# Each engine takes the stages of five software-pipelined streams in its own order

## The chip, the cores and the metric

The kernel runs on one core of a Trainium2 chip. The metric is the device time of one execution in microseconds, lower is better; the time before is the median of three runs. The core has five engines with a queue each: TensorE (PE, matmuls into PSUM), VectorE (DVE), ScalarE (ACT), GpSimd (POOL, and issuer of some DMAs) and SyncE (SP, issuer of most DMAs). They meet only through semaphores.

## The reference

Two transformer layers over x of shape (16, 256, 256). With `xn = layernorm(x)`:

```
layer 0: x = x + attention(xn) (16 heads of 16, causal, x @ w_qkv, softmax, @ w_out)
               + qffn(xn)      (W = (codes - 128) * scale; down(silu(gate) * up), hidden 704)
layer 1: x = x + latent attention(xn) (16 heads, latent 64 with its own layernorm, causal softmax)
               + moe(xn)       (32 experts of 96, top 6 of sigmoid scores, and a shared expert of 192)
```

## The kernel before

One element of the batch (256 tokens by 256) is the unit of work; there are 16. Its work is cut into stages, and five streams of stages run at once, each on another element. In a steady run `it` they are, with the digit that selects them in the string:

- 0, `xx1(it)`, layer 0, 44 stages: `stack` (DVE copies the stacked query and key parts), `q0` to `q7` (score rows for the row maxima), `f0` to `f2` (quantised ffn chunks), `q8` to `q15`, `max`, `f3` to `f5`, `dn5`, `k0` to `k15` (scores again, exponentials, weighing), `w3`, `t1`, `end`.
- 1, `xx2(it-1)`, layer-1 attention and router, 31 stages: `O1` (turn the loaded layer-0 attention output), `OP` (output projection, new x), `LN`, `X` (turn the normalised x), `GRAM` (and router logits), `K`, `RS` (and values), `ROUTER`, `COMB` (turn and store the expert weights), `LOAD`, `Q0` to `Q7` (two score rows each), `MAX`, `K0` to `K7` (two key rows each), `W3`, `T1`, `O`, `PROJ`.
- 2, `xx3(it-2, last_units)`, the experts' later half: gates `g`, ups `u` and downs `d` of units 7 to 13, then `OUT`. "Older" in what follows, written `<g8`.
- 3, `xx3(it-1, first_units)`, units 0 to 6 ("newer", `>g0`); unit 0 and 1 are the shared expert, and `>wt` is the stage in which GpSimd broadcasts the expert weights with 12 DMAs.
- 4, `xx0(it+1)`, layer 0's front, 6 stages: `ln1`, `x` (turn), `qq`, `kk`, `v`, `land` (SP loads the stacked parts).

`xx` is `sp`, `gp`, `act`, `dve` or `pe`. Each of these is a Python generator that emits its engine's part of a stage and yields. A stage may be empty on an engine. `run` walks the string and calls `next` on the stream that each digit names; what it emits lands in the engine's queue in that order:

```
def run(layer1, layer0, older, newer, front, order="body"):
    streams = (layer0, layer1, older, newer, front)
    for turn in ORDERS[order]:
        if streams[int(turn)] is not None:
            next(streams[int(turn)], None)
```

There are five strings of 125 digits, one for each kind of run: `start` (it 0, with the last weight pieces and folding as streams 2 and 3), `first` (it 1), `body` (it 2 to 14, 13 runs), `late` and `end`. All five engines use the same string.

PSUM is what ties the engines together: two banks for stream 0 and 4 (`ring1`), two for stream 1 (`ring2`), two for the experts (`ring3`, bank 0 for gates and bank 1 for ups), and two accumulators. TensorE fills a bank, ScalarE, VectorE or both empty it. An expert unit goes PE gate, ACT tanh (L921), DVE product (L1224), POOL times the broadcast weights (L712), PE up, DVE product (L1219), ACT high half (L917), POOL low half (L721), PE down (L1341). SP's `>g0` loads `xe`, once the older stream's last up is done; GpSimd's `>g0` adds the bias into `xbe` (L698), once SP has stored the `xbe` of the element before (L555, stage `<OUT`).

Of the kernel before, what the change touches and what calls it, by code (L numbers as in the profile page):

```python
# [65 lines left out]
def prev(it):  # L66

    if isinstance(it, int):
# [11 lines left out]
ORDERS = {  # L80
    "body": ("022022100112201001002102212122210122022201021021211111031030201023100101011011301000043303"
             "41000040303043003433043310303331033"),
    "start": ("202021002020010013011200020010000020122110001302003330310110014122403301020123243321233111"
             "00413013103132204412213010313230110"),
    "first": ("001001210022121001310311210200003200131101012010310221013031012311321013114201302300100401"
             "20300400224122000324203204303330332"),
    "late": ("042220120012120421011220121220021224202201111114210212131020301020131330013014310011010300"
             "03300303000003034000001000333133331"),
    "end": ("200001021210212120122441220400012200212221040022020110001110002001021131423031021330101304"
             "11300101310331333133031003000330303"),  # L90
# [3 lines left out]
def program(nc, a, out):  # L94
# [22 lines left out]
    with ctx:  # L117
# [442 lines left out]
        def _(sp):  # L560
# [71 lines left out]
            run(None, None, None, None, front)  # L632
            for i in range(NSLOT, NCODE):
                load_codes(i)
            run(None, sp1(sp, 0), convert(1, EARLY), None, sp0(sp, 1), order="start")
            run(sp2(sp, 0), sp1(sp, 1), convert(EARLY, len(pieces)), sp3(sp, 0, first_units), sp0(sp, 2), order="first")
            for it in range(2, B - 1):
                run(sp2(sp, it - 1), sp1(sp, it), sp3(sp, it - 2, last_units), sp3(sp, it - 1, first_units), sp0(sp, it + 1))
            run(sp2(sp, B - 2), sp1(sp, B - 1), sp3(sp, B - 3, last_units), sp3(sp, B - 2, first_units), None, order="late")
            run(sp2(sp, B - 1), None, sp3(sp, B - 2, last_units), sp3(sp, B - 1, first_units), None, order="end")  # L640
            run(None, None, sp3(sp, B - 1, last_units), None, None)
# [84 lines left out]
        def _(gp):  # L726
# [37 lines left out]
            run(None, None, None, None, gp0(gp, 0))  # L764
            run(None, gp1(gp, 0), convert(1, EARLY), None, gp0(gp, 1), order="start")
            run(gp2(gp, 0), gp1(gp, 1), convert(EARLY, len(pieces)), gp3(gp, 0, first_units), gp0(gp, 2), order="first")
            for it in range(2, B - 1):
                run(gp2(gp, it - 1), gp1(gp, it), gp3(gp, it - 2, last_units), gp3(gp, it - 1, first_units), gp0(gp, it + 1))
            run(gp2(gp, B - 2), gp1(gp, B - 1), gp3(gp, B - 3, last_units), gp3(gp, B - 2, first_units), None, order="late")
            run(gp2(gp, B - 1), None, gp3(gp, B - 2, last_units), gp3(gp, B - 1, first_units), None, order="end")  # L770
            run(None, None, gp3(gp, B - 1, last_units), None, None)
# [154 lines left out]
        def _(act):  # L926
# [24 lines left out]
            run(None, None, None, None, front)  # L951
# [13 lines left out]
            run(None, act1(act, 0), convert(1, EARLY), folding(), act0(act, 1), order="start")  # L965
            run(act2(act, 0), act1(act, 1), convert(EARLY, len(pieces)), act3(act, 0, first_units), act0(act, 2), order="first")
            for it in range(2, B - 1):
                run(act2(act, it - 1), act1(act, it), act3(act, it - 2, last_units), act3(act, it - 1, first_units), act0(act, it + 1))
            run(act2(act, B - 2), act1(act, B - 1), act3(act, B - 3, last_units), act3(act, B - 2, first_units), None, order="late")
            run(act2(act, B - 1), None, act3(act, B - 2, last_units), act3(act, B - 1, first_units), None, order="end")  # L970
            run(None, None, act3(act, B - 1, last_units), None, None)
# [258 lines left out]
        def _(dve):  # L1230
# [75 lines left out]
            run(None, None, None, None, front)  # L1306
# [18 lines left out]
            run(None, dve1(dve, 0), convert(1, EARLY), folding(), dve0(dve, 1), order="start")  # L1325
            run(dve2(dve, 0), dve1(dve, 1), convert(EARLY, len(pieces)), dve3(dve, 0, first_units), dve0(dve, 2), order="first")
            for it in range(2, B - 1):
                run(dve2(dve, it - 1), dve1(dve, it), dve3(dve, it - 2, last_units), dve3(dve, it - 1, first_units), dve0(dve, it + 1))
            run(dve2(dve, B - 2), dve1(dve, B - 1), dve3(dve, B - 3, last_units), dve3(dve, B - 2, first_units), None, order="late")
# [423 lines left out]
```

## Time and profile before

| | before |
|---|---|
| median of 3 runs | 2086.21 us (2081.82 to 2092.85) |
| profiled execution | 2090.68 us |
| its span, first to last instruction | 2088.9 us |
| mean granted clock of TensorE | 0.971 |
| TensorE, VectorE, GpSimd, ScalarE busy | 84%, 53%, 42%, 39% |
| one steady run | about 121 us |
| bytes moved by DMA | 139.26 MB, 67 GB/s |

A busy share is the union of an engine's recorded instructions. Matmuls are recorded with their pipeline, so that neighbours overlap. A granted clock of 1.00 is full speed.

### The profile page before, as it was taken

To read this page: it belongs to the slowest core of one execution; us is meant where nothing else is said; L and a number is where in the kernel's file an instruction comes from. 1 tells how busy PE (TensorE), PEld (TensorE's weight loads), DVE (VectorE), ACT (ScalarE), POOL (GpSimd) and SP (SyncE) were. 2 spreads that over 40 slices of the span, in tenths; PEclk is the share of its full clock that TensorE was granted. 3 is DMA by queue.
4 is the path that set the end of the run, shared out by engine and by line. 5 is a ranking of instruction groups with operands and counts; after the bars stand their busy time and mean duration, and the time that the engine had idled before them with its cause. 6 is when DMAs were issued, how large, how long until landed. Compare 5 with 4: busy or idle time off the path is not lost.

```text
span 2088.9 us, 41844 instructions
## 1 busy us (share of the span) xinstructions
PE 1758.0 (84%) x16112; PEld 1337.9 (64%) x16112; DVE 1108.2 (53%) x2557; ACT 822.3 (39%) x1598; POOL 875.5 (42%) x995
## 2 busy tenths in 40 slices
PE   3647888889898888989888898988889898888887
PEld 2424666757676575766767576776757677676666
DVE  5546373645547365563736556473645547364432
ACT  2433425343342534334353433425343343534432
POOL 2323334534354353435435343534534353443445
PEclk7778999999999999999999999999999999999999
DMA  6532212313141231314123141412313141321111
GB/s 142 132 91 60 69 44 70 73 49 74 40 94 50 65 72 55 74 40 93 50 68 75 49 74 40 98 45 75 68 48 74 45 104 40 81 56 44 52 57 36
DMA packets 323318, 139.26 MB, mean 67 GB/s; under 512 B 227568, under 2 KB 308528, under 8 KB 323120
## 3 DMA queue, kind: packets, MB, share of 16 engines
q1 hardware_dynamic: 304688, 86.23, 18.2%
q0 software_dynamic: 18432, 50.36, 9.0%
q8 instruction: 128, 2.10, 0.4%
q14 instruction: 70, 0.57, 0.1%
HBM read 102.12 MB, written 29.88 MB: 63 GB/s over the span
## 4 chain that ended last, share of the span: by engine, by line
PE 29%; DVE 23%; ACT 13%; issue 12%; POOL 10%; SPq 7%; DMA 5%; DVEq 0%; POOLq 0%; ACTq 0%
PE s3r L1344 7%; POOL gs L712 4%; SPq L529 3%; POOL cb L691 3%; DVE th L1219 3%; DVE gs L1224 3%; PE s2acc L1341 3%; ACT p L826 2%; DVE m L1174 2%; PE s2r L1559 2%; PE s1a L1344 2%; ACT th L921 2%; POOL h2l L721 2%; PE s1acc L1447 2%; ACT p L886 2%
## 5 line engine op out<-in xcount | busy, mean ns | idle before, releaser
L721 POOL TENSOR_TENSOR h2l<-th,h2h 128x512 f16<-128x512 f32 (+1 forms) x224 | 246.8, 1102 | 388.6 <-ACT h2h L917 385.2
L712 POOL TENSOR_TENSOR gs<-gs,cb 128x512 f32<-128x512 f32 x192 | 243.4, 1268 | 309.8 <-DVE gs L1224 306.2
L917 ACT CAST h2h<-th 128x512 f16<-128x512 f32 (+1 forms) x224 | 131.6, 588 | 542.4 <-DVE th L1219 501.1
L1344 PE MATMUL s3r<-xe,xg 128*128 128x256 f16 x2304 | 285.3, 274 | 1.6 <-DVE gs L1224 0.5
L1344 PE MATMUL s3r<-xe,xu 128*128 128x256 f16 x2304 | 283.6, 273 | 0.4 <-DVE th L1219 0.4
L1341 PE MATMUL s2acc<-xd,h2h 128*128 128x256 f16 x1536 | 264.7, 274 | 13.5 <-POOL h2l L721 13.5
L1224 DVE SCALAR_TENSOR_TENSOR gs<-th,s3r 128x512 f32<-128x512 f32 (+1 forms) x224 | 144.9, 647 | 234.8 <-ACT th L921 234.3
L1344 PEld LDWEIGHTS s3r<-xe,xg 128*128 128x128 f16 x2304 | 223.5, 98 | 38.3 <-issue 6.6
L1344 PEld LDWEIGHTS s3r<-xe,xu 128*128 128x128 f16 x2304 | 225.6, 98 | 27.3 <-DVE th L1219 1.0
L691 POOL DMA_DIRECT2D cb<-comb_d x384 | 227.6, 600 | 20.3 <-issue 10.6
L1219 DVE TENSOR_TENSOR th<-s3r,gs 128x512 f32<-128x512 f32 x192 | 132.4, 690 | 170.9 <-POOL gs L712 157.4
L1341 PE MATMUL s2acc<-xd,h2l 128*128 128x256 f16 x768 | 210.7, 274 | 0.0
L921 ACT ACTIVATE th<-s3r 128x512 f32<-128x512 f32 (+1 forms) x224 | 126.3, 564 | 199.8 <-PE s3r L1344 198.1
L1341 PEld LDWEIGHTS s2acc<-xd,h2h 128*128 128x128 f16 x1536 | 148.7, 98 | 38.3 <-POOL h2l L721 20.1
L1174 DVE TENSOR_REDUCE m<-s2r 128x3 f32<-128x384 f32 x256 | 130.8, 551 | 14.0 <-PE s2r L1561 8.2
L886 ACT ACTIVATE p<-s2r 128x384 f32<-128x384 f32 x256 | 111.1, 486 | 62.7 <-PE s2r L1605 62.7
L656 POOL TENSOR_TENSOR h1p<-th,h1p 128x256 f16<-128x256 f32 x96 | 64.4, 670 | 130.4 <-ACT h1p L814 129.7
L1559 PE MATMUL s2r<-stacks 126*128 126x128 f16 (+1 forms) x512 | 85.6, 253 | 29.5 <-DVE m L1174 13.5
L698 POOL TENSOR_TENSOR xbe<-x,bo_row 128x512 f32<-128x512 f32 x16 | 21.8, 1364 | 199.3 <-DMA out<-xbe 199.3
L1052 DVE TENSOR_REDUCE mx<-s1b 128x2 f32<-128x512 f32 x128 | 87.1, 681 | 16.8 <-PE s1b L1423 16.8
L826 ACT ACTIVATE p<-s1b 128x512 f32<-128x512 f32 x128 | 76.6, 599 | 44.7 <-PE s1b L1466 38.9
L1052 DVE TENSOR_REDUCE mx<-s1a 128x2 f32<-128x512 f32 x128 | 87.1, 681 | 10.8 <-PE s1a L1423 10.8
(280 smaller groups left out, 3157.6 us busy)
## 6 DMA issues: line engine op xcount, KB each, us to landing
cb<-comb_d POOLq DMA_DIRECT2D x128, 192.0 KB, 3.4
part_d<-part SPq DMA_DIRECT2D x32, 512.0 KB, 3.2
cb<-comb_d POOLq DMA_DIRECT2D x128, 128.0 KB, 3.1
stacks<-part_d SPq DMA_DIRECT2D x192, 64.0 KB, 2.4
va<-v_d SPq DMA_DIRECT2D x512, 8.0 KB
cb<-comb_d POOLq DMA_DIRECT2D x128, 64.0 KB, 3.1
land<-part_d SPq DMA_DIRECT2D x96, 64.0 KB, 2.7
part<-part_d SPq DMA_DIRECT2D x96, 64.0 KB, 4.0
```

Of the source, the lines that this page charges most:

```text
L691: gp.dma_start(dst, src[which, 2 * group:2 * group + 2].partition_broadcast(32 * count)).then_inc(sem(f"cb2_loaded{group % 2}"), 16)
L712: g.tensor_tensor(gc2[:, p % 2, :], gs2[:, p % 2, :], cb2[:, 2 * (p % 6):2 * (p % 6) + 2, :].rearrange("p a s -> p (a s)"), ALU.mult).then ...
L721: g.tensor_tensor(h2l[0:m, n % 2, 0:w], th2[0:m, n % 2, 0:w], h2h[0:m, n % 2, 0:w], ALU.subtract).then_inc(sem("h2l_made"), 1)
L886: s.activation(p2[:, i % PSLOT, :], ring2[u % 2][:, 0:3 * P], ACT.Exp, scale=L ** -0.5).then_inc(empties2(u), 1)
L917: s.copy(h2h[0:m, n % 2, 0:w], th2[0:m, n % 2, 0:w]).then_inc(sem("h2h_made"), 1)
L921: s.activation(th2[0:m, n % 2, 0:w], ring3[0][0:m, 0:w], ACT.Tanh, scale=0.5).then_inc(sem("th2_made"), 1)
L1052: v.tensor_reduce(mx1[:, h, :], two(bk), AX.X, ALU.max).then_inc(empties1(u), 1)
L1174: v.tensor_reduce(m32[:, h, :], bk[:, 0:3 * P].rearrange("p (c n) -> p c n", n=P), AX.X, ALU.max).then_inc(empties2(u), 1)
L1219: ins = v.tensor_tensor(th2[0:m, s, 0:w], bk[0:m, 0:w], gc2[0:m, s, 0:w], ALU.mult)
L1224: v.scalar_tensor_tensor(gs2[0:m, s, 0:w], th2[0:m, s, 0:w], 1.0, ring3[0][0:m, 0:w], ALU.add, ALU.mult).then_inc(empties3(0), 1)
L1341: ins = nc.tensor.matmul(bk, lhs[i][k], rhs[j][k], start=first and chain[0], stop=last and chain[1], skip_group_check=True)
L1344: ins = nc.tensor.matmul(bk, lhs[i][k], rhs[j][k], start=first, stop=last)
```

## The change

`ORDERS` gets a level above: a dictionary of the five strings for each engine, and `run` takes the engine's name. Every string still has each digit as often as before (44, 31, 23, 21 and 6 times), so each stream's own stages keep their sequence; only how the streams interleave on one engine changes, separately for each. Stages, waits, buffers and transfers are the same.

```
-def run(layer1, layer0, older, newer, front, order="body"):
+def run(engine, layer1, layer0, older, newer, front, order="body"):
     streams = (layer0, layer1, older, newer, front)
-    for turn in ORDERS[order]:
+    for turn in ORDERS[engine][order]:
...
-    "body": ("022022100112201001002102212122210122022201021021211111031030201023100101011011301000043303"
-             "41000040303043003433043310303331033"),
+  "pe":  "body": ("022020012122001121002101022221120220212100142212101012131301200103100101031101310120001003"
+                  "34300300403040003043343303001333133"),
+  "dve": "body": ("020202011120012120010212122020212212012102021211120121130103001100001000303003010112100002"
+                  "44033040340330331030314303310333431"),
...
```

The body string in stage names, as far as an engine has work in the stage. Before, all engines (stages with TensorE work, then VectorE's):

```
PE  <g7 <u7 q0 <d6 <g8 O1 q1 q2 OP <u8 <d7 q3 X q4 q5 GRAM q6 q7 <g9 K f0 <u9 <d8 RS <g10 <u10 <d9 <g11 COMB f1 <u11 <d10 f2 <g12 <u12
    <d11 q8 Q0 q9 <g13 Q1 q10 <u13 Q2 <d12 Q3 Q4 Q5 Q6 Q7 q11 >g0 MAX q12 >u0 q13 <d13 q14 K0 q15 >g1 K1 max f3 K2 f4 K3 f5 K4 K5 dn5
    K6 K7 >u1 k0 W3 k1 k2 k3 k4 >d0 k5 >g2 x T1 k6 k7 k8 k9 qq k10 >u2 k11 >d1 k12 kk >g3 k13 k14 >u3 v >d2 >g4 k15 >u4 >d3 O w3 >g5 t1
    >u5 >d4 >g6 PROJ >u6 >d5
DVE stack <g7 <u7 q0 <g8 O1 q1 q2 OP LN <u8 q3 X q4 q5 GRAM q6 q7 <g9 K f0 <u9 RS <g10 ROUTER <u10 <g11 f1 <u11 f2 <g12 <u12 q8 Q0 q9
    <g13 Q1 q10 <u13 Q2 Q3 Q4 Q5 Q6 Q7 q11 >g0 MAX q12 >u0 q13 q14 q15 <OUT >g1 max f3 f4 f5 dn5 K7 >u1 ln1 >g2 x T1 qq >u2 k12 kk ...
```

After, each engine's own:

```
PE  <g7 <u7 q0 <d6 q1 q2 O1 <g8 OP <u8 <d7 q3 q4 X <g9 GRAM q5 q6 <u9 K q7 RS f0 <d8 <g10 <u10 <d9 COMB <g11 f1 <u11 <d10 f2 <g12 <u12
    Q0 q8 q9 Q1 <d11 <g13 Q2 <u13 Q3 q10 Q4 q11 Q5 <d12 Q6 >g0 Q7 >u0 q12 MAX <d13 q13 q14 K0 q15 >g1 K1 max f3 K2 f4 K3 f5 >u1 K4 K5 dn5
    K6 K7 k0 W3 k1 k2 k3 T1 k4 k5 >d0 >g2 x >u2 k6 k7 >d1 k8 k9 qq k10 >g3 k11 kk k12 k13 k14 >u3 k15 v >d2 >g4 >u4 >d3 w3 >g5 t1 O
    >u5 >d4 >g6 PROJ >u6 >d5
DVE stack <g7 q0 <u7 q1 q2 O1 OP LN <g8 q3 q4 X <u8 GRAM q5 q6 K q7 <g9 RS <u9 ROUTER <g10 f0 <u10 f1 <g11 <u11 f2 Q0 <g12 Q1 q8 <u12
    q9 Q2 <g13 Q3 Q4 Q5 <u13 q10 Q6 Q7 MAX >g0 q11 q12 >u0 q13 q14 q15 max f3 f4 f5 dn5 >g1 >u1 K7 <OUT ln1 x >g2 qq k12 >u2 kk ...
ACT ... <g9 K RS <u9 <g10 f0 COMB <u10 f1 <g11 f2 <u11 ... (before: <g9 K f0 <u9 RS <g10 <u10 <g11 COMB f1 <u11 f2)
POOL ... <u13 f3 f4 f5 dn5 >g0 >u0 >u1 >wt >g2 ... (before: <u13 >g0 >u0 f3 f4 f5 dn5 >u1 >wt >g2)
SP  ... COMB LOAD >g0 q8 q9 q10 q11 q12 q13 MAX q14 q15 max ln1 <OUT kk ... (before: COMB LOAD q8 to q11 >g0 MAX q12 to q15 <OUT max ln1 kk)
```

## Rows read from the trace of the kernel before

**Rows 1.** The page's totals: busy time, share of the span and instructions of each engine.
```profile
PE 1758.0 (84%) x16112; PEld 1337.9 (64%) x16112; DVE 1108.2 (53%) x2557; ACT 822.3 (39%) x1598; POOL 875.5 (42%) x995
```

**Rows 2.** Stretches of the span, first two and last from the edges, middle steady.
```profile
core 0: us, PE busy (x) PEld busy (x) DVE busy (x) ACT busy (x) POOL busy (x), PEclk, DMA share, GB/s
0.00:152.50 152.50, 76.86 (x463) 47.40 (x464) 78.30 (x170) 55.10 (x90) 39.55 (x43) 0.75 0.53 125
152.50:276.60 124.10, 99.36 (x870) 71.80 (x869) 68.71 (x156) 47.30 (x93) 43.44 (x52) 0.92 0.23 59
...
962.39:1083.43 121.04, 106.69 (x1004) 82.00 (x1004) 66.42 (x155) 49.23 (x97) 52.55 (x60) 1.00 0.27 65
...
1930.00:2050.00 120.00, 103.58 (x961) 80.65 (x962) 50.33 (x119) 43.98 (x83) 58.00 (x66) 0.99 0.19 54
```

**Rows 3.** TensorE's waits in seven steady runs: total us, times, longest.
```profile
PE s2r L1580 <- ACT p L886: 15.6, 14, 1.2
PE s2r L1547 <- DVE cm L1166: 12.3, 7, 1.8
PE s2r L1344 <- DVE part L1096: 7.7, 7, 1.4
PE s1b L1464 <- DVE x1l L1021: 6.9, 7, 1.0
PE s1a L1421 <- DVE kst L1041: 6.7, 7, 1.0
PE s2r L1344 <- DVE part L1110: 5.9, 7, 0.8
...
PE s1acc L1447 <- ACT p L826: 4.5, 14, 0.4
...
PE s2r L1350 <- DVE xn L996: 3.7, 7, 0.5
PE s2r L1559 <- DMA stacks<-part_d: 3.6, 7, 0.9
PE s2r L1602 <- DMA stacks<-mt: 2.8, 7, 0.7
```

**Rows 4.** TensorE in a steady run, in order of time: start, length, instruction.
```profile
1024.13 1.47 PE L1344 MATMUL s3r<-xe,xg 128*128 128x256 f16 x12
1025.44 1.47 PE L1344 MATMUL s3r<-xe,xu 128*128 128x256 f16 x12
...
1031.03 0.33 PE L1559 MATMUL s2r<-stacks 126*128 126x128 f16 x2
...
1031.31 0.33 PE L1559 MATMUL s2r<-stacks 126*128 126x128 f16 x2
...
1069.89 0.39 PE L1341 MATMUL s2acc<-shd,h2h 128*128 128x256 f16 x2
```

**Rows 5.** VectorE in the same steady run, in order of time.
```profile
1014.63 0.67 DVE L1224 SCALAR_TENSOR_TENSOR gs<-th,s3r 128x512 f32<-128x512 f32 x1
...
1034.61 6.53 DVE L1174 TENSOR_REDUCE m<-s2r 128x3 f32<-128x384 f32 x12
...
1046.78 0.68 DVE L1207 TENSOR_TENSOR xbe<-s2acc,xbe 128x512 f32<-128x512 f32 x1
...
1062.54 0.62 DVE L1010 TENSOR_TENSOR xn<-s2r,rc 128x64 f32<-128x64 f32 x4
```

**Rows 6.** GpSimd in the same steady run, in order of time.
```profile
1050.72 1.27 POOL L698 TENSOR_TENSOR xbe<-x,bo_row 128x512 f32<-128x512 f32 x1 [14.15 <-DMA out<-xbe]
1051.95 0.67 POOL L721 TENSOR_TENSOR h2l<-th,h2h 128x256 f16<-128x256 f32 x1
...
1066.45 7.15 POOL L691 DMA_DIRECT2D cb<-comb_d  x12
```

**Rows 7.** DMA issues of SP: count, size, median us to landing.
```profile
xe<-part SPq DMA_DIRECT2D x16, 256.0 KB, 2.4
out<-xbe SPq DMA_DIRECT2D x16, 256.0 KB, 2.2
```

More of the change, by code:

```diff
@@ L80 @@
 ORDERS = {
-    "body": ("022022100112201001002102212122210122022201021021211111031030201023100101011011301000043303"
-             "41000040303043003433043310303331033"),
[L83 to L88, printed above, removed]
@@ new lines @@
+    "pe": {
+        "body": ("022020012122001121002101022221120220212100142212101012131301200103100101031101310120001003"
+                 "34300300403040003043343303001333133"),
+        "start": ("200201120110120100000311100022002402000120001030001130103323023312204102130041332101330121"
+                 "01243103103221023312234302140103101"),
+        "first": ("022010021102100103021222321110030200120031110101301010130210103121131301110103201033401024"
+                 "32002004201204200303043402003323323"),
+        "late": ("022212010204014222120101000212201222121202210211103121114023410300301011001003131343243011"
+                 "00100300100300100300300003033331333"),
+        "end": ("201402014122212100022001212002201021201022402020140420001002110001003131000100201321310431"
+                 "31031331313103313023001301303013330"),
+    },
@@ new lines @@
+    "act": {
+        "body": ("022201120101200122100122021011210221002022210010121123202131130010021012011130101300104030"
+                 "34000040040303034403333300310333331"),
+        "start": ("002220101022010020003110200000201121000101002023001130011301301413322411010313201031410323"
+                 "03131122340113212220034133020303204"),
+        "first": ("221100001212131020010121003221111020210030120001100300230121123011131210213213020120413003"
+                 "04120000243023204001004334003033333"),
+        "late": ("212000120022001100221102221212210222201100122001413212101311023110430314000411320311010400"
+                 "03330100040301003003001033333133030"),
+        "end": ("100222211121102212412201120221202202214141000211103203124304410010103000000310100301311200"
+                 "00233301000333133001130030303031300"),
+    },
@@ new lines @@
+    "gp": {
+        "body": ("002122114002200422020210202012222420011102201410002100020010033434003303301301203301011200"
+                 "11101313013300210013333311013103101"),
+        "start": ("201201132403211000002003030011103000213020023310400420300021123210111022010131304121010241"
+                 "03100010312231302131110024032333022"),
+        "first": ("220013020000101220013432200030012112011400011121001211002131210300003114210031313102002400"
+                 "02323002132340030312132313340302011"),
+        "late": ("201000400221000212112120422221212402212121211022203120210100031013001403043303303330031010"
+                 "03103310000130100004311311000303113"),
+        "end": ("202020020220122022001020020012021012241121222313000112333000101033101313030010031030241014"
+                 "13100340341033011200134331131100001"),
+    },
@@ L950, in _ @@
             piece(0)
-            run(None, None, None, None, front)
+            run("act", None, None, None, None, front)
             for i in range(NCODE):
@@ L1305, in _ @@
             v.tensor_scalar(centre[:, :], ident[0:L, 0:L], 1.0 / L, None, ALU.subtract).then_inc(sem("dve_const"), 1)
-            run(None, None, None, None, front)
+            run("dve", None, None, None, None, front)
             for i in range(NCODE):
@@ L1674, in _ @@
             pe.wait_ge(*event("acc_cleared", None, 2))
-            run(None, None, None, None, pe0(pe, 0))
+            run("pe", None, None, None, None, pe0(pe, 0))
             for i in range(NCODE):
```

89 lines of the change are left out of this document (55 added, 34 removed).

## The prediction

> **What bounds the kernel now.** I read the engine totals first, then the busy time run by run, then TensorE's waits in the steady runs, and only then the order of instructions around each wait. TensorE leads with 84% [rows 1]. Single runs say more: a steady run takes 121.04 us, in which TensorE is busy 106.69 us, VectorE 66.42, GpSimd 52.55 and ScalarE 49.23, at a granted clock of 1.00, the 2.4 GHz level [rows 2]. Thirteen such runs are 1,573 us of the 2088.9, so the body string decides nearly everything. TensorE is the bound, but 121.04 - 106.69 = 14.35 us of each run it stands still, and only that can be won by an order, since no instruction is added or removed. The waits of seven steady runs tell what it stands for: the ten rows shown make 69.7 / 7 = 10.0 us per run in pieces of 0.4 to 2.2, so no one chain holds TensorE [rows 3]. So the question is, place by place, whether the new string puts more ready work between a producer and TensorE's need of it, and what it delays in exchange.
>
> Some prices serve all of it. One expert pass (gate, up or down, twelve matmuls) holds TensorE 1.31 us, the distance of two such starts, 1024.13 and 1025.44; a layer-1 query row (half a stage) holds it 0.28 us, the distance of 1031.03 and 1031.31; a layer-0 row is three matmuls, about 0.33 us by a quarter of 1.31 [rows 4]. A 512-column VectorE step takes 0.67 us [rows 5].
>
> **The change part by part, body run.** No stage gets a new wait, DMA or table load; every number below is a changed distance.
>
> COMB. TensorE waits 12.3 / 7 = 1.76 us for the router's weights [rows 3]. VectorE now does the router before older gate 10, not after: 0.67 us earlier [rows 5]; it also does ffn 0 (two steps of half the columns, 0.7 us) after it. TensorE has between RS and COMB: before, gate 10, up 10, down 9, gate 11, 4 x 1.31 = 5.2 us; after, ffn 0 (eight matmuls, 0.87), down 8, gate 10, up 10, down 9, 6.1 us. Sum: 0.67 + 0.7 + 0.9 = 2.3 us of room against a wait of 1.76. I count the whole 1.76 as gone.
>
> OP. It waits 7.7 / 7 = 1.10 us for the low part of O1 [rows 3]. Before, two layer-0 query rows (0.66 us) lie between O1 and OP; after, older gate 8 (1.31). Gain 0.65; I add 0.2 since VectorE no longer does gate 8 ahead of O1: 0.85.
>
> X and GRAM. X waits 3.7 / 7 = 0.53 for the layernorm and gets a second query row in front (0.33): gain 0.33. GRAM waits 5.9 / 7 = 0.84 [rows 3]; the two query rows (0.66) in front of it become gate 9 (1.31): gain 0.65. Against them, VectorE now does OP and the whole layernorm before older gate 8, and TensorE's gate 9 needs that bank. Up 8, down 7, q3, q4 and X cover 3.8 us; the new x (0.68), the layernorm of nine short steps (an estimate of 3 us, between four and five full steps) and the product (0.67) take 4.4: loss 0.3 with X's remaining wait counted as cover.
>
> x (front). The key row behind it waits 6.9 / 7 = 0.99 for its low part [rows 3]. Newer up 2 (1.31) moves between them and the turn T1 (four matmuls, 0.45) moves away, to between k3 and k4: gain 0.75 there and, since T1, down 1 and kk now stand before the fourth, eighth and twelfth key rows, most of the 4.5 / 7 = 0.64 for the exponentials: 0.4.
>
> The query block. This is the one stretch where VectorE sets the pace: it takes twelve maxima without a gap in 6.53 us, 0.54 each, while TensorE needs 0.28 per row [rows 4, 5]. Q3 to Q7 stand back to back in the old string, and five stages cost TensorE 10 x 0.54 = 5.4 us instead of 2.8. In the new one q10, q11, down 12 and newer gate 0 are strewn among them, and VectorE does the older output sum and newer gate 1 and its step after this stretch (0.69 + 0.4 us less in it). I read 1.1 us from what leaves VectorE here and 0.4 from the load wait of 3.6 / 7 = 0.51 [rows 3], since ScalarE copies COMB before gate 11, not after: 1.5 together. The most it could be is 2.6 + 0.5.
>
> Costs. MAX to K0: before q12, up 0, q13, down 13, q14 cover (3.1 us), after only down 13, q13, q14 (2.0), with a wait there already of 2.8 / 7 = 0.40 [rows 3]; VectorE answers sooner by q11 and gate 0 (about 0.5): loss 0.6. Newer gate 0 needs a load that SP issues after older up 13; it lands 2.4 us after its issue [rows 7], and the cover shrinks from 7 to about 4 us: loss 0.2. On SP that issue now stands ahead of the value loads of q8 to q15, sixteen DMAs that nobody needs before k0. The output sum moves on VectorE behind K7 and its store on SP behind the load of x: GpSimd's xbe, idle 14.15 us for it, runs later, and newer down 0 waits for GpSimd. Worked out from rows: the tail of K7 ends at 1062.54 + 0.62, the sum takes 0.68, the store 2.2 to land, xbe 1.27, the low part 0.67: 1068.0, and 0.9 more estimated for the hops between four queues, 1068.9, against down 0 at 1069.89 [rows 4 to 7]: it fits with 1.0 us to spare, less as TensorE gets faster: loss 0.3. Twelve broadcasts of 7.15 us follow on GpSimd [rows 6], 4 us later than now, and gate 2's product after them; newer up 2 of VectorE then ends about where it ends now. Unchanged stay the two pair waits of 15.6 / 7 = 2.23 us and the turn behind them, which lie inside one stage, and the 0.96 us for the stack copies at the start, ahead of which the VectorE work does not shrink [rows 3].
>
> Sum: 1.76 + 0.85 + 0.33 + 0.65 + 0.75 + 0.4 + 1.5 = 6.2, less 0.3 + 0.6 + 0.2 + 0.3 = 1.4: 4.8 us. A removed stall also removes cover from the next chain, so I take 4.0 per run. Bounds: above, the whole idle time of 14.35 less the 2.23 and 0.96 that stay, 11.2 us; below, nothing, or a loss if the costs grow to the 3 us that the late GpSimd chain could add. Times 13: 52 us, bounds 145 and -40.
>
> **The edges.** In the window that holds the end of the start run and most of the first one TensorE idles 24.7 us of 124.1, in the first 152.5 us 75.6, in the one over the end run 16.4 of 120 [rows 2]. In the start run VectorE's piece 10 (1.7 us) leaves the path ahead of ffn 3 and two ffn stages move ahead of the fold; in the first run SP starts the load of O1 before the values. I take 3 us for the start, 3 for the first, 2 each for late and end: 10, bounds 0 and 25.
>
> Total 62 us. The profiled execution took 2090.68, so 2028.7; it lay 4.5 us above the median of 2086.21, which gives **2024 us**, 3% faster.
>
> **A page on this sum.** The sum above prices the query block by starts, not by busy time. The Trainium skill (Perfetto Trace Analysis, Identifying the Most-Contended Engine) says that matmul busy time is a bad measure of headroom, because matmuls are pipelined, and that weight-load busy share is better. This trace agrees in the block: a row's matmuls are recorded 0.33 us long and the next row starts 0.28 us after it [rows 4]. By that rule the idle share is not 14.35 of 121 but up to 39 us (82.00 busy loading weights [rows 2]), which makes the next-but-one rival likelier, not the forecast.
>
> **The rivals.**
> (a) Waits only change place. TensorE's stalls are small because some chain always comes due; with four other engines each in its own order the next due chain takes over. Then a run keeps 120.5 to 121 and the time is 2075 to 2087. For it: the waits are many and small [rows 3]. Against: VectorE, ScalarE and GpSimd are each idle over 45% of a run [rows 2], so there is slack to give.
> (b) Much more comes back: each moved stage wins its full wait, and the hidden gaps of back-to-back rows too. 7 us per run, 91, and 20 at the edges: 1975. For it: the weight-load share. Against: 2.23 us lie inside stages and 0.96 ahead of all of it [rows 3].
> (c) Slower: the late output chain. If xbe on GpSimd comes over 1.0 us late, newer down 0 stalls; each further us is lost once per run, and the gates behind the twelve broadcasts with it. It turns the whole gain of 4.8 around at 5.8 us late, for example when SP's store has to queue behind a late load of x, which itself waits for y1. At 8 us late: 13 x 2.2 = 29 slower, 10 back at the edges, 2105.
> (d) The change does nothing, because an engine's real order is set by waits anyway: 2086. Against: the order in a queue does bind here, GpSimd stood 14.15 us before xbe with the ffn chunks of the same run queued behind it [rows 6], so I give it little.
>
> **How the numbers follow.** Forecast (2000 to 2060) 0.62; (b) 0.14; (a) and (d) 0.12, half of it within 0.5%; (c) 0.12. A measurement here tells about 0.5% from no change. Faster 0.62 + 0.14 + 0.06 = 0.82, same 0.07 with a part of (c), slower 0.11. The range leaves out most of (c) and the lower half of (b): 1982 to 2072.
>
> **What would show it.** Steady runs of 116 to 118 us with the same busy counts; COMB's wait under 0.3 us per run, those of OP, GRAM and the x row under 0.5; the stack-row wait and the pair waits as they are; VectorE's maxima no longer twelve in a row; MAX-to-K0 wait near 1 us. Wrong it would be if a wait on GpSimd's low parts or on the store appears at newer down 0 (c), or if the waits add up to 13 us again under other names (a).

## The result and the profile after

The changed kernel takes 2019.47 us, median of 4 runs (2017.58 to 2021.59), against 2084.79 for the kernel before on the same chip (4 runs): a ratio of 0.969, 95% interval 0.966 to 0.9715. The profiled execution took 2017.58 us with a span of 2015.8. The forecast was 2024. Lines of the kernel stand 50 further down than before (L1344 is L1394, L1041 is L1091).

Totals of the page, then a steady run, to be read against [rows 1] and [rows 2]:

```profile
PE 1746.5 (87%) x16112; PEld 1333.6 (66%) x16112; DVE 1100.9 (55%) x2557; ACT 819.5 (41%) x1596; POOL 874.7 (43%) x995
```

```profile
core 0: us, PE busy (x) PEld busy (x) DVE busy (x) ACT busy (x) POOL busy (x), PEclk, DMA share, GB/s
947.78:1063.99 116.21, 106.03 (x1004) 81.99 (x1003) 65.65 (x156) 49.09 (x97) 52.62 (x60) 1.00 0.27 67
```

The work is the same, 1004 matmuls in a run, and what shrank is nearly all standing still: 116.21 - 106.03 = 10.2 us instead of 14.35. The starts of VectorE's first stack copy divide the span into runs. Before, the first and the last of the fourteen starts that enclose the thirteen body runs:

```profile
251.56 0.41 DVE L1041 COPY qst<-land 48x512 f32<-48x512 f32 x1
...
1833.45 0.41 DVE L1041 COPY qst<-land 48x512 f32<-48x512 f32 x1
```

After:

```profile
247.61 0.41 DVE L1091 COPY qst<-land 48x512 f32<-48x512 f32 x1
...
1769.24 0.41 DVE L1091 COPY qst<-land 48x512 f32<-48x512 f32 x1
```

Thirteen runs went from 1581.9 to 1521.6 us: 60.3 us, 4.6 for each. The part ahead of them lost 4.0 us, the part behind them (255.4 to 246.6) 8.9. So four fifths of the difference between these two executions is the body string. They differ by 73.1 us, the medians by 65.3: the profiled execution of before was 5.9 us above its median, so single executions tell such parts only to a few us.

TensorE's waits in seven steady runs, the view of [rows 3] (total, times, longest):

```profile
PE s2r L1630 <- ACT p L936: 15.5, 21, 1.1
PE s2acc L1391 <- POOL h2l L771: 6.9, 15, 0.6
PE s1a L1471 <- DVE kst L1091: 6.8, 7, 1.0
PE s2r L1619 <- DVE mx L1228: 4.5, 7, 0.6
...
PE s2r L1394 <- DVE part L1146: 3.9, 7, 0.6
PE s2r L1609 <- DMA stacks<-part_d: 3.0, 4, 1.0
PE s2r L1652 <- DMA stacks<-mt: 2.8, 7, 0.4
...
PE s2r L1582 <- DVE xn L1173: 2.7, 7, 0.5
...
PE s1a L1394 <- ACT p L876: 2.4, 7, 0.3
PE s2r L1394 <- DVE part L1160: 2.0, 7, 0.3
...
PE s2r L1400 <- DVE xn L1046: 1.2, 6, 0.2
```

The wait at COMB, the second row of [rows 3], is gone from the list, and so are x1l and the `s1acc` row. The pair weighing and the stack copies stand as they did (15.5 and 6.8, before 15.6 and 6.7). OP fell from 1.10 to 0.56 us per run, GRAM from 0.84 to 0.29, X from 0.53 to 0.17. New are 0.63 us at MAX, and GpSimd's low parts at the older down 7 (0.59) and down 9 (0.30). New too are 0.39 us at RS (L1582), which now stands ahead of ffn 0 and down 8, and 0.34 at `kk` (`s1a` L1394), and 0.20 each at the value product behind RS and at older gate 11. By the two full lists, the waits that shrank or went make 6.4 us per run, those that are new or grew 2.5.

Where in the run the standing went. TensorE's instruction at the start of each of three stretches is the same in both kernels: the first row of layer 0 (`q0`), the router's weights (COMB), the first key row of layer 1 (K0), and then the next run's `q0`. First before, then after, columns as above:

```profile
989.46:1018.66 29.20, 24.24 (x231) 20.18 (x231) 22.25 (x55) 9.65 (x18) 14.02 (x16) 1.00 0.22 60
1018.66:1045.08 26.42, 24.97 (x216) 19.29 (x216) 19.27 (x39) 6.65 (x14) 9.78 (x9) 1.00 0.16 45
1045.08:1110.50 65.42, 57.49 (x557) 42.54 (x558) 24.89 (x64) 32.93 (x65) 28.75 (x35) 1.00 0.34 75
```

```profile
951.88:976.71 24.83, 22.64 (x218) 19.07 (x219) 19.73 (x52) 9.48 (x17) 10.88 (x12) 1.00 0.25 67
976.71:1004.33 27.62, 26.15 (x231) 20.41 (x229) 20.98 (x42) 6.87 (x15) 12.93 (x13) 1.00 0.17 44
1004.33:1068.10 63.77, 57.25 (x557) 42.52 (x557) 24.95 (x64) 32.74 (x65) 28.81 (x35) 1.00 0.33 77
```

TensorE stands still 4.96, 1.45 and 7.93 us in them before, 2.19, 1.47 and 6.52 after. The middle stretch, which holds the query block, gave nothing; it is longer only because older gate 11 (1.31 us) moved into it.

The late output chain, which answers to the last rows of [rows 4] to [rows 6], on VectorE, GpSimd and TensorE:

```profile
1022.33 0.68 DVE L1257 TENSOR_TENSOR xbe<-s2acc,xbe 128x512 f32<-128x512 f32 x1
```

```profile
1025.39 1.27 POOL L748 TENSOR_TENSOR xbe<-x,bo_row 128x512 f32<-128x512 f32 x1 [3.96 <-DMA out<-xbe]
1026.62 1.29 POOL L771 TENSOR_TENSOR h2l<-th,h2h 128x256 f16<-128x256 f32 x2
```

```profile
1029.19 0.38 PE L1391 MATMUL s2acc<-shd,h2h 128*128 128x256 f16 x2
```

The sum ends at 1023.0, its store has landed by 1025.39, the first of GpSimd's two low parts (1.29 us together) ends at about 1027.3, and newer down 0 starts at 1029.19 with no wait beside it: 1.9 us to spare.

### The profile page after: what moved, and what is told of

Read it like the earlier page. It is cut to its first block, busy times and chain, and to the rows that moved or that the text cites. A ratio compares the mean times of both kernels' runs of the same rounds, so it can differ in the third digit from the quotient of the medians.

```text
span 2015.8 us, 41842 instructions
## 1 busy us (share of the span) xinstructions
PE 1746.5 (87%) x16112; PEld 1333.6 (66%) x16112; DVE 1100.9 (55%) x2557; ACT 819.5 (41%) x1596; POOL 874.7 (43%) x995
## 4 chain that ended last, share of the span: by engine, by line
PE 26%; issue 25%; DVE 19%; POOL 17%; ACT 8%; SPq 3%; DMA 2%; POOLq 0%; DVEq 0%; ACTq 0%
PE s3r L1394 7%; POOL gs L762 6%; POOL h2l L771 5%; POOL cb L741 3%; PE s2acc L1391 3%; DVE th L1269 3%; DVE mx L1102 3%; PE s1a L1394 2%; DVE gs L1274 2%; PE s2r L1394 2%; PE s1acc L1497 2%; POOL h1p L706 2%; PE s1a L1514 2%; ACT h2h L967 1%; ACT p L876 1%
## 5 line engine op out<-in xcount | busy, mean ns | idle before, releaser
L771 POOL TENSOR_TENSOR h2l<-th,h2h 128x512 f16<-128x512 f32 (+1 forms) x224 | 246.5, 1103 | 390.9 <-ACT h2h L967 380.5
L1394 PE MATMUL s3r<-xe,xg 128*128 128x256 f16 x2304 | 284.5, 273 | 2.7 <-DVE gs L1274 2.7
L1394 PE MATMUL s3r<-xe,xu 128*128 128x256 f16 x2304 | 283.0, 273 | 1.6 <-DVE th L1269 1.6
L1394 PEld LDWEIGHTS s3r<-xe,xg 128*128 128x128 f16 x2304 | 222.7, 98 | 39.9 <-DVE gs L1274 8.7
L1394 PEld LDWEIGHTS s3r<-xe,xu 128*128 128x128 f16 x2304 | 223.7, 98 | 31.6 <-DVE th L1269 5.5
L864 ACT CAST h1p<-th 128x256 f16<-128x256 f32 x96 | 38.8, 404 | 154.4 <-DVE th L1138 154.4
L876 ACT ACTIVATE p<-s1a 128x512 f32<-128x512 f32 x128 | 76.7, 599 | 45.1 <-PE s1a L1516 43.7
```

The lines of the kernel that those rows point to most:

```text
L771: g.tensor_tensor(h2l[0:m, n % 2, 0:w], th2[0:m, n % 2, 0:w], h2h[0:m, n % 2, 0:w], ALU.subtract).then_inc(sem("h2l_made"), 1)
L876: s.activation(p1[:, n % PSLOT, :, :], two(bk), ACT.Exp, scale=HD ** -0.5).then_inc(empties1(u), 1)
L1394: ins = nc.tensor.matmul(bk, lhs[i][k], rhs[j][k], start=first, stop=last)
```

## The experiments

All ratios are to the kernel before, run beside it on the same chip. The experiments ran on several chips, on which the kernel before took 2084.8 to 2089.8 us, so ratios are to be compared and not medians. "Thirteen runs" is the distance between the two stack copies shown above, from the one profiled execution of each kernel.

| kernel | median us | ratio (95%) | thirteen runs us |
|---|---|---|---|
| before | 2084.79 | 1 | 1581.9 |
| changed | 2019.47 | 0.9688 (0.966 to 0.9715) | 1521.6 |
| 1 body strings alone | 2024.49 | 0.9686 (0.9665 to 0.9706) | 1518.4 |
| 2 edge strings alone | 2080.69 | 0.9961 (0.9943 to 0.9978) | 1588.8 |
| 3 one string for all engines | 2198.48 | 1.0525 (1.0502 to 1.0548) | 1699.5 |
| 4 COMB as before | 2044.95 | 0.9784 (0.9765 to 0.9804) | 1546.2 |
| 5 query rows in one block | 2042.72 | 0.9792 (0.9773 to 0.9811) | 1544.9 |
| 6 output sum as before | 2019.6 | 0.9679 (0.9659 to 0.9699) | 1523.7 |
| 7 pair stages divided | 2013.46 | 0.9651 (0.9631 to 0.9671) | 1516.9 |
| 8 output sum later still | 2122.15 | 1.017 (1.0151 to 1.0189) | 1626.6 |
| 9 = 7, with O1 earlier on TensorE | 2012.78 | 0.9654 (0.9641 to 0.9667) | 1516.4 |
| 10 MAX later on VectorE | 2023.38 | 0.9704 (0.969 to 0.9717) | 1525.3 |
| 11 one string for ScalarE and VectorE | 2279.93 | 1.0939 (1.0922 to 1.0955) | 1791.8 |
| 12 = 9, with OP's whole chain earlier | 2011.04 | 0.9629 (0.9608 to 0.9651) | 1509.9 |

The diffs are in stage names, one engine's body string to a line; RTR is ROUTER.

**1. Body strings alone.**

```
 each engine: "body" as in the changed kernel
-             "start", "first", "late", "end" of the changed kernel
+             "start", "first", "late", "end" of the kernel before
```

> New body strings on all five engines, the strings of start, first, late and end as before. Theory A (the gain is one of distance, so much per steady run): the runs go from 121.3 to 116.7 us, 13 of them, about 60 us less than before, ratio 0.971. Theory B (the body strings only fit behind the new start and first strings, because each run inherits the lag between the engines from the one before it): the first three or four body runs stay at 119 us or more, and less than 45 us are left of the gain, ratio 0.978 or above.

The whole gain is there, 0.9686 against 0.9688, as the first theory had it. The runs take 116.0 to 118.2 us from the first on; in the changed kernel the first takes 117.8 and the last, next to the new late string, 121.0.

**2. Edge strings alone.**

```
-"body" of the changed kernel
+"body" of the kernel before, for every engine
```

> Old body string on all engines, new strings for start, first, late and end. Theory A: 13 us less than before (4 ahead of the second run, 9 behind the thirteenth body run, as the two traces show), ratio 0.994. Theory B (lags are inherited, also from the edges into the body): the body runs change as well, and the ratio lies outside 0.991 to 0.997.

0.4% by itself, some 8 us, with the interval clear of 1; but 1 shows that on top of the new body nothing of it can be measured. The two parts outside the body lost the 13 us that were expected (3.4 ahead, 9.6 behind), but the thirteen runs, with the old string, took 6.9 us more than in the profile of before, so the second theory can't be ruled out: part of what the edges win may come back in the body. One execution of each can't tell that from chance.

**3. One string for all five engines**, TensorE's new one, with the stages in which TensorE has no work put where the old string had them.

```
-each engine: its own body string
+all engines: s0 <g7 <u7 q0 <d6 q1 q2 O1 <g8 OP LN <u8 ... (TensorE's, with LN behind OP, RTR behind RS, LOAD behind f1,
+             ln1 behind k3, <OUT behind q15, >wt behind W3)
```

> All five engines take TensorE's new body string (stages that are empty on TensorE put where they stood before: output sum after q15, broadcasts after W3, load after f1, ln1 after k3); edges as in the changed kernel. Theory A (freedom of each engine is what pays: VectorE must defer old gates to the layernorm and the low parts of ups, GpSimd its ffn chunks): most of the 4.6 us per run is lost, steady runs of 119.5 to 121, ratio 0.983 to 0.994. Theory C (a better order of TensorE's own stages is what pays, one string would have done): runs of 117 to 118, ratio 0.970 to 0.978.

It is 5% slower than the kernel before, some 8.6% slower than the changed kernel, and much worse than anything expected. TensorE's waits in seven runs:

```profile
...
PE s1b L1514 <- DVE th L1060: 16.0, 7, 2.3
PE s3r L1394 <- DVE gs L1274: 15.0, 7, 2.1
PE s1a L1514 <- ACT p L876: 12.3, 14, 1.5
```

And the longest wait of VectorE there, with the same row of the changed kernel's seven runs behind it:

```profile
DVE gs L1274 <- ACT th L971: 121.5, 84, 4.2
```

```profile
DVE gs L1274 <- ACT th L971: 43.2, 28, 2.2
```

VectorE stands before a gate's product 84 times instead of 28, for ScalarE's activation, which has only just been given the same place in its own queue. So TensorE's order is good only while the others are not in it. That is shown for this one string; whether a single string that was sought for all five engines together would reach a part of the gain was not tried, nor was TensorE's new string with the old one left to the other four.

**4. COMB as before:** ffn 0 and the down ahead of RS, gates 10 and 11 ahead of COMB.

```
-pe: K q7 RS f0 <d8 <g10 <u10 <d9 RTR COMB <g11 f1        dve: <g9 RS <u9 RTR <d8 <g10 f0 <u10 f1 <d9 COMB <g11
+pe: K q7 f0 <d8 RS <g10 <u10 <d9 <g11 RTR COMB f1        dve: <g9 f0 <u9 <d8 RS <g10 RTR <u10 <d9 <g11 COMB f1
 (act and gp: the same stages back in the old sequence)
```

> The changed kernel with the old local order between K and gate 11 in the body on TensorE (f0 and down 8 ahead of RS, COMB behind gate 11), VectorE (router behind gate 10), ScalarE (COMB behind gate 11) and GpSimd (ffn 0 ahead of up 9). Theory A (the terms of the sum add up): the router wait of 1.76 us per run comes back, 13 times, 23 us more than the changed kernel, ratio about 0.980. Rival (waits only change place): the next chain takes up most of it, under 8 us more, ratio under 0.973.

```profile
PE s2r L1609 <- DMA stacks<-part_d: 12.0, 7, 1.8
PE s2r L1597 <- DVE cm L1216: 10.4, 7, 1.5
```

The wait for the router's weights (`cm`) is back, 10.4 / 7 = 1.5 us, and 12.0 / 7 = 1.7 behind it for the key loads instead of 0.4. The thirteen runs take 24.6 us more than in the changed kernel, 1.9 each; by the ratios it is 20 us in all, 1.5 each. That is no price of COMB alone: besides the 1.5 and the 1.3 for the loads 0.6 us come at an ffn stage (`s1b` L1444), while the new waits at RS, the value product, gate 11 and down 9 go (0.39, 0.20, 0.20, 0.30). What it shows is the cause: the place of the router stages decides the wait for `cm`, and most of it comes back when they are put back.

**5. Query rows in one block.**

```
-pe: <u13 Q3 q10 Q4 q11 Q5 <d12 Q6 >g0 Q7 >u0 q12 MAX     dve: Q3 Q4 Q5 <u13 q10 Q6 <d12 Q7 MAX
+pe: <u13 <d12 Q3 Q4 Q5 Q6 Q7 q10 q11 >g0 >u0 q12 MAX     dve: <u13 <d12 Q3 Q4 Q5 Q6 Q7 q10 MAX
```

> The changed kernel with Q3 to Q7 back to back again in the body, on TensorE (then q10, q11, newer gate 0, up 0) and on VectorE. Theory A: VectorE paces the block and the gap of TensorE comes back, 1.0 to 1.5 us per run, 13 to 20 us more than the changed kernel, ratio 0.975 to 0.978. Rival (VectorE has the same work in the stretch either way and TensorE only waits elsewhere in it, at MAX): under 5 us, ratio under 0.972.

```profile
PE s2acc L1391 <- POOL h2l L771: 14.6, 22, 1.1
PE s2r L1609 <- DVE m L1224: 8.6, 28, 0.7
```

The thirteen runs take 23.3 us more, 1.8 each (22 us by the ratios). The waits for VectorE's maxima are back (8.6 / 7 = 1.2, before 0.76), those at MAX and at the load of `mt` (0.63 and 0.40) are gone, and the earlier down 12 waits 1.1 us for GpSimd. So this is a third order and not the old one: from COMB to the first key row a steady run takes 29.07 us here, 27.62 in the changed kernel, and 26.42 + 1.31 = 27.73 before, with gate 11 counted in. The 1.8 us are the price of this order, and the predicted gain of 1.5 is not what they measure.

**6. Output sum as before** (VectorE's older down 13 and output sum behind q15; SP's store and GpSimd's newer gate 0 and up 0 put back to match).

```
-dve: K7 k6 k7 k8 k9 <OUT ln1         gp: <u13 f3 f4 Q1 f5 dn5 >g0 >u0
+dve: q15 <d13 <OUT max ...           gp: <u13 >g0 >u0 f3 f4 Q1 f5 dn5
```

> The changed kernel with the older output sum back behind q15 on VectorE, its store back ahead of max on SP, and GpSimd's newer gate 0 and up 0 back ahead of f3. Theory A (the late output costs nothing, and VectorE gets 0.7 us less in the stretch in which it paces): 0.3 to 0.7 us per run lost, 4 to 9 us more than the changed kernel. Rival (the late GpSimd chain cost something that it now gives back): as much faster. Third: exactly the same, since the stretch ends at MAX and not at max: within 2 us.

The same time within the interval. The move of the output chain that I had priced at 0.3 us per run, 4 us in all, is too small for these intervals (0.966 to 0.9715 and 0.9659 to 0.9699); all that can be said is that it cost and gave no more than some us.

**7. Pair stages divided:** each of the two stages that hold a pair of key rows and the weighing behind it becomes two, with another stream's stage between.

```
-pe: K2 f4 K3 f5 >u1 K4 K5                  act: K2 f4 K3 <OUT f5 K4 K5
+pe: K2 f4 K2b K3 f5 K4 >u1 K4b K5          act: K2 f4 K2b K3 <OUT f5 K4 K4b K5
 in layer 1's generator: "yield" before "if n in (4, 8): weigh(...)"
```

> The changed kernel with one more yield in TensorE's and ScalarE's stages K2 and K4, between the pair of key rows and the weighing that needs their exponentials; in the body f4 stands between the two halves of K2 and newer up 1 between those of K4. Theory A (the two waits inside a stage, 1.1 and 0.6 us per run, are the price of the stage's cut and not of the chain): 1.2 to 1.7 us per run less, 16 to 22 us under the changed kernel, ratio 0.958 to 0.961. Rival (ScalarE then holds the weighed sum longer, and the next key row waits for its bank instead): within 5 us of the changed kernel.

```profile
PE s2r L1631 <- ACT p L936: 6.1, 14, 0.6
PE s2r L1653 <- ACT pr L943: 5.7, 14, 0.6
```

The waits for the exponentials fell from 15.5 to 6.1, but 3.8 came back one step later at `pr` (1.9 to 5.7), and 0.7 at the ffn's low part from GpSimd (2.8 to 3.5). Counted from stack copy to stack copy, the experts' low parts from GpSimd wait as in the changed kernel (6.8 us in seven runs), and TensorE waits 3.4 us, in four pieces, for the load at O1, where 9 shows only 0.2. Net 4.7 us in thirteen runs, some 8 us by the ratios, whose intervals still overlap: at most half of what was expected, and near the rival. A removed wait is given back in part, seen row by row.

**8. Output sum later still:** behind the layernorm of the next x on VectorE.

```
-dve: <OUT ln1
+dve: ln1 <OUT
```

> The changed kernel with VectorE's older output sum moved behind ln1, so some 8 us later in each body run (1030.2 for 1022.3). It tests the slower rival's price. In the trace of the changed kernel GpSimd's low part for newer down 0 is done at 1027.3 and TensorE needs it at 1029.2: 1.9 us to spare. If the chain is what the rival says, each run loses 8 less 1.9, about 6 us: 75 us slower than the changed kernel, ratio about 1.005, and the wait stands at newer down 0. If TensorE can make it up later in the run (the chain is hidden further down), under 40 us.

This was meant to price the slower rival. GpSimd's xbe and TensorE's newer down 0 in one run:

```profile
1078.65 1.26 POOL L748 TENSOR_TENSOR xbe<-x,bo_row 128x512 f32<-128x512 f32 x1 [11.77 <-DMA out<-xbe]
```

```profile
1080.60 0.61 PE L1391 MATMUL s2acc<-shd,h2h 128*128 128x256 f16 x2 [5.78 <-POOL h2l L771]
...
1081.85 2.17 PE L1394 MATMUL s3r<-xe,xg 128*128 128x256 f16 x12
```

TensorE stands 5.8 us here, as computed, and over seven runs 49.0 us instead of 6.9 for this row, 6.0 more in each. But each run grew by 8.1 us and the kernel by about 100, not 75. The difference is the clock: twelve matmuls behind the stall are recorded 2.17 us long instead of 1.47 [rows 4], and over the thirteen runs TensorE is busy 1408.1 us with the 13045 matmuls that take 1382.7 in the changed kernel, 2.0 more in each. The windows around the stall, granted clock in the column PEclk:

```profile
1070.00:1080.00 10.00, 4.20 (x51) 2.12 (x40) 2.43 (x9) 6.30 (x10) 1.35 (x2) 0.99 0.08 28
1080.00:1090.00 10.00, 9.40 (x78) 6.74 (x79) 1.28 (x2) 3.62 (x7) 9.47 (x15) 0.84 0.48 154
1090.00:1100.00 10.00, 9.50 (x93) 7.53 (x92) 3.54 (x9) 5.14 (x11) 2.14 (x2) 1.00 0.19 57
```

Ten us at 0.84 instead of 1.00 are 1.6 us lost. Behind the thirteen stalls of this trace (eleven of 5.8 us, two of 7.6 and 7.7) the ten us have 0.67 to 0.84, 2.3 us lost on average.

**9. O1 one query stage earlier on TensorE**, on top of 7.

```
-pe: q1 q2 O1 <g8 OP
+pe: q1 O1 q2 <g8 OP
```

> Edit: the kernel with the divided pair stages, and TensorE alone takes O1 between the query stages 1 and 2 of layer 0 instead of behind both, so that the down of O's merge has one more query stage (0.7 us) between O1 and OP. Theory A (the 0.56 us that OP still waits in each run is the split of O1's result on VectorE, the shape of the wait as before): OP's wait falls from 0.56 to 0.1 to 0.3 us in each run and O1's own operands are there, 0.2 to 0.4 us in each of 16 runs, some 3 to 6 us below the kernel with the divided stages: 2008 to 2011 us. Theory B (O1 is itself only just supplied: its input lands by a transfer that the kernel with divided stages already waited 1.3 us for in some runs): the wait moves from OP to O1, and the time is that of the kernel with divided stages, 2013 to 2016 us.

The time is that of 7 (0.9654 and 0.9651), as the rival has it, but not for the rival's reason: OP still waits, up to 0.56 us in six of seven runs, and O1's own input only 0.2 us, once. In this kernel ScalarE's copy for O1 runs at 951.98, right behind the older up 7's cast at 951.46, which waited for VectorE's th (950.73), which waited 0.85 us for GpSimd:

```profile
950.73 0.69 DVE L1270 TENSOR_TENSOR th<-s3r,gs 128x512 f32<-128x512 f32 x1 [0.85 <-POOL gs L762]
```

```profile
951.46 0.62 ACT L968 CAST h2h<-th 128x512 f16<-128x512 f32 x1 [4.47 <-DVE th L1270]
951.98 0.58 ACT L896 CAST part<-s2r 128x512 f16<-128x512 f32 x1
```

So the wait at OP was set on ScalarE's queue: its copy starts no sooner, and VectorE's low part behind it (952.66) no sooner either, though O1 came a query stage earlier on TensorE.

**10. MAX behind layer 0's query stage 11 on VectorE**, meant to bring the copy at MAX out of GpSimd's addition.

```
-dve: Q7 MAX >g0 q11
+dve: Q7 q11 MAX >g0
```

> Edit: VectorE alone takes its step for query head 11 of layer 0 (a 0.67 us reduction) ahead of MAX instead of behind it; all else is the changed kernel. Theory A (the MAX wait of 0.63 us in each run is there because VectorE's 128x16 copy runs beside GpSimd's addition of 1.16 us, and takes 0.82 us where it took 0.18 us before): the copy now begins when GpSimd's addition is all but over, and takes 0.18 us; with 0.67 us more ahead of it and 0.64 us less in it, the wait of TensorE at MAX stays at 0.6 to 0.7 us and the time is the same, 2019 to 2021 us. Theory B (the copy is long for what VectorE does just before it, in the kernel itself): it stays at 0.82 us, TensorE waits 1.2 to 1.3 us at MAX, and the time is some 10 us longer, 2029 us.

The edit did not do what I said: the copy belongs to the last step of Q7, not to MAX, and stood where it was, beside the same addition, at 0.81 us. Only the row behind it came late (the load of `mt` waits 6.8 / 7 = 1.0 us instead of 0.4), 0.3 us per run. The time is within the interval of the changed kernel's. It tells nothing of the copy; 12 repeats the question.

**11. One string for ScalarE and VectorE only**, the string of 3; the others keep their own.

```
-act, dve: their own body strings
+act, dve: the one string of experiment 3
```

> Edit: ScalarE and VectorE take the body in TensorE's own order (the one string of the third experiment); TensorE, GpSimd and SyncE keep their own orders of the changed kernel. Theory A (the 10 us in each run that one string for all five engines cost arise where VectorE and ScalarE hand to each other and to TensorE: ScalarE's sigmoid input and VectorE's product stand at one place of the same string, so neither runs ahead): most of the loss comes back with these two alone, runs of 121 to 126 us, 2090 to 2150 us. Theory B (it is the transfers and GpSimd's late halves that need their own order): with those two free, the runs are near 117 to 119 us, 2025 to 2045 us.

Runs of 135 to 142 us, worse than when all five shared the string, and outside both expectations. Two of TensorE's waits in seven runs:

```profile
PE s1a L1514 <- ACT p L876: 27.9, 14, 6.0
PE s2r L1609 <- DVE m L1224: 24.5, 21, 2.4
```

They make 7.5 us per run, for ScalarE's exponentials of layer 0 and for VectorE's maxima. A part of the loss is the clock again: TensorE is busy 1463.3 us in the thirteen runs with the matmuls that take 1382.7 in the changed kernel, at a mean granted clock of 0.95 instead of 1.00. Two engines out of step with three cost more than five in step, so a share of the 8.6% can't be given to an engine by this run; which engine's freedom carries how much stays open.

**12. OP's whole chain**, on top of 9: O1 earlier on ScalarE and VectorE too, older down 7 behind q3 and q4, and q11 ahead of Q7 on VectorE, so that the copy starts later.

```
-act: <g7 <u7 <d6 q0 O1      dve: q2 O1 / <d12 Q7 MAX >g0 q11      pe: <g8 OP <u8 <d7 q3 q4
+act: <g7 O1 <u7 <d6 q0      dve: O1 q2 / <d12 q11 Q7 MAX >g0      pe: <g8 OP <u8 q3 q4 <d7
```

> Edit: the kernel with the divided pair stages and O1 ahead of query stage 2, and with it: ScalarE takes its copy for O1 ahead of the older up 7, VectorE its part of O1 ahead of query stage 2, TensorE the older down 7 behind query stages 3 and 4 instead of ahead of them, and VectorE its reduction for query stage 11 ahead of the last reduction for the pair rows (it now stands before the 128x16 copy, which the tenth experiment failed to bring about). Theory A (OP waited because ScalarE's copy for O1 stood behind the older up 7, whose cast waited through VectorE for GpSimd's addition; the 0.58 us at the older down 7 are GpSimd's late half, behind its four DMA issues): OP's 0.56 us go, the older down 7, 0.66 us later by the two query stages and 0.56 us earlier by OP, waits 0.4 to 0.6 us still or less, so that 0.6 to 1.0 us go in each of 13 runs of the body: 2000 to 2006 us. Theory B (the wait at the older down 7 takes up what OP gives back and layer norm's X waits for the rest): under 0.3 us in each run, 2009 to 2013 us. On the copy, by its own rows: theory A (it can't end while GpSimd's addition of 1.16 us runs) 0.2 to 0.4 us, since it begins shortly before that addition ends, and ends with it; theory B (it is long by itself) 0.82 us. TensorE's wait at MAX is 0.5 to 0.8 us under A and about 1.3 us under B, since the reduction ahead of the copy adds 0.6 us.

OP's wait is gone from the list; older down 7 waits 0.66 us, X and GRAM as in 9, and the load of `mt` 0.8 instead of 0.4, since MAX comes behind q11. The thirteen runs take 6.5 us less than in 9, 0.5 each. The ratio of 0.963 is the lowest of all, but its interval overlaps that of 9, and the profiled execution spent 4.5 us more ahead of the body, where the two kernels have the same strings. So it is ahead of the changed kernel by 0.6%, of 9 not surely. The time lies in the range of theory B, though the wait at OP went as theory A had it: the older down 7 (0.66 for 0.58) and the load of `mt` (0.84 for 0.40) took back nearly all of OP's 0.56 us. A part of the 6.5 may be chance, since the wait for the key rows' loads, which the edit leaves alone, is 2.4 us less in seven runs. The copy:

```profile
996.51 0.43 DVE L1228 COPY mx<-m 128x16 f32<-128x16 f32 x1
```

```profile
995.75 1.16 POOL L771 TENSOR_TENSOR h2l<-th,h2h 128x512 f16<-128x512 f32 x1 [5.06 <-ACT h2h L968]
```

It ends at 996.94, GpSimd's addition at 996.91.

## Why the prediction was right

**The bound, and where the gain comes from.** Right. TensorE's busy time stayed (106.69 to 106.03; over the thirteen runs 1385.6 to 1382.7), and its idle time fell, by 4.2 us in the run shown and by 4.4 on average. Over all thirteen runs a run is 4.6 us shorter, so 60 us and not 52. The mechanism, distance between a producer and TensorE's need of it, and the size of the sum are right. The parts are not all right, and this is a piece of luck:

| stretch of TensorE, mean of seven runs | before | after | won | predicted |
|---|---|---|---|---|
| `q0` to COMB (gate 11's 1.31 us taken off before) | 27.7 | 24.8 | 2.9 | 3.3 |
| COMB to the first key row (gate 11 taken off after) | 26.7 | 26.7 | 0.0 | 0.7 |
| first key row to the next `q0` | 65.2 | 63.7 | 1.5 | 0.85 |

**The terms.** COMB: the wait of 1.76 went whole, as predicted, but the move brought waits of 0.39 us at RS and 0.20 at the value product, which the sum put at nothing. X and GRAM: 0.33 and 0.65 predicted, 0.36 and 0.55 by the waits. OP: 0.85 predicted, 0.54 measured; 9 and 12 show why: I counted what lies between O1 and OP on TensorE, while ScalarE's copy in between stood behind an older cast. The front's x row and the weighing: 0.75 and 0.4 predicted; both rows of [rows 3] are gone, 0.99 and 0.64, so 0.5 more, of which 0.34 came back at `kk`.

The query block is the term that failed. I had 1.5 us for it, 1.1 of them for the maxima and 0.4 for the load of the key rows. By the wait lists the maxima gave 0.76 and the load wait 0.1 (3.6 to 3.0 in seven runs), and 0.63 at MAX and 0.20 at gate 11 took all of it back: the stretch that holds the block has the same standing as before, 1.47 us against 1.45. VectorE still takes its maxima in rows of six and four there, with other steps between them, and is busy 20.98 of 27.62 us. Experiment 5 does not measure this term, since its order is slower than the old one too.

**The costs.** MAX to K0: I had 0.6 us more at the load of `mt`; that wait stayed at 2.8 / 7, and 0.63 us came one step earlier, at MAX itself, by a cause that I had not seen (below). The right size, then, by the wrong mechanism. The late output: 0.3 predicted, no wait at newer down 0; 1.9 us were left where I had 1.0. Gate 9: 0.3 predicted, no wait there, 0.2 at gate 11. The load for newer gate 0: 0.2 predicted, no wait. Not in my list: 0.59 and 0.30 us at the older downs 7 and 9, which now come before GpSimd's low part, and the waits at RS, the value product and `kk`. My costs of 1.4 and the 0.8 us that I took off for such new waits make 2.2, against 2.5 measured, and the removed waits 6.2 against 6.4: both totals are near, but they rest on other places than I named, above all in the last stretch.

**The edges.** 10 us predicted. The profiled span shows 12.9 outside the body runs, experiment 2 some 8 by itself, but 1, with the old edges, is as fast as the changed kernel. Kernels that share the new edge strings differ by 4.5 us in the stretch ahead of the body (246.5 to 251.0), and in 2 the body runs took 6.9 us more. So 0 to 8 us is all that can be said, and the 10 is not confirmed.

**The rivals.** That waits only change place did not happen, though it holds piecemeal: 7 gave back half or more of what it removed, and the query block all. The slower rival's mechanism is real. Experiment 8 lets it happen and adds 5% to the changed kernel, with a stall of 5.8 us in each run. By my rule that would have cancelled the gain and 1 us per run more; the kernel of 8 is 3.4 us per run and 1.7% in all slower than before, since the clock adds about a third to the stall. The larger gain did not come: the weight loads fill 82 of 116 us, which by the reading behind that rival leaves 34 us, while the best of the later orders found another 1 us in a run. These were a few changes by hand, so they set no bound.

## What to carry to other kernels

When several streams share in-order queues, let each engine have its own order, and check each pair's distance on every queue that the value passes: the wait at OP was seen on TensorE, stayed when O1 moved there alone, and went when ScalarE and VectorE took their parts of it earlier. An order is good only together with those of the other engines; the same TensorE order with the others forced into it was 5% slower than the kernel before. Count removed waits from the wait list, and take off a good third for new ones (here 2.5 us against 6.4 removed). Check a term by the time between two fixed instructions around its stretch, and not by undoing it alone: here a removed wait of 0.8 us in the query block was worth nothing, and experiment 5 seemed to say 1.8. Look for the chain with the least spare time, since a stall of some 6 us costs its length and a slower clock behind it.

## What the runs showed of the hardware

**A VectorE copy beside a GpSimd addition.** The copy of 128x16 values at MAX takes 0.18 us before, when GpSimd is idle, and 0.82 us after, in each of the thirteen body runs:

```profile
1041.17 0.18 DVE L1177 COPY mx<-m 128x16 f32<-128x16 f32 x1
```

```profile
1000.28 0.82 DVE L1227 COPY mx<-m 128x16 f32<-128x16 f32 x1
```

```profile
999.92 1.16 POOL L771 TENSOR_TENSOR h2l<-th,h2h 128x512 f16<-128x512 f32 x1 [5.07 <-ACT h2h L967]
```

The addition ends at 1001.08, the copy at 1001.10. In 12, where it starts 0.40 us before the addition's end, it takes 0.43; in 5, where no addition runs beside it, 0.18. In all thirteen runs of the changed kernel and of 12 the copy ends 0.02 to 0.04 us after the addition. So it does not run at a part of its speed; it waits until GpSimd's instruction is over, and GpSimd's is not longer for it (1.15 before). The Trainium skill (Trainium Architecture — The Big Picture, What this means for kernel authors) says that the SBUF port pair shared by VectorE and GpSimd is an exclusive lock and no split of bandwidth; the traces of the changed kernel and of 12 agree. The same shows in the stack copies at the start of each run, two groups of four alike:

```profile
947.78 2.48 DVE L1091 COPY qst<-land 48x512 f32<-48x512 f32 x4
950.29 1.53 DVE L1091 COPY kst<-part 48x512 f32<-48x512 f32 x4
```

```profile
948.59 1.38 POOL L771 TENSOR_TENSOR h2l<-th,h2h 128x512 f16<-128x512 f32 x1 [1.52 <-ACT h2h L967]
```

The group with the addition beside it takes 0.95 us longer, and here the addition too is longer, 1.38. The kernel before has the same there (2.49 us beside an addition of 1.39). TensorE waits 0.96 us for these copies in each run, in both kernels; whether another place of the addition would remove it was not tried.

**The clock behind a stall.** After TensorE stood 5.8 us in experiment 8, the granted clock was 0.84 over the next 10 us (0.67 to 0.84 behind the thirteen stalls of that trace), against 0.99 and 1.00 on either side of this one, and the first matmuls of 256 columns started 0.2 us apart instead of 0.11, the 1.2 GHz level instead of 2.4. The waits of up to 1.8 us in the steady runs of before left it at 1.00 [rows 2, 3].
